# A decoder's mixture-of-depths stage in four sets with side work beside its units, and unread identity products on TensorE

## The reference

```
x = x + L0_attn(ln(x))        # causal self-attention, 16 heads of 16
x = x + L0_xattn(ln(x), ctx)  # cross-attention on 64 context rows
x = x + L0_ffn(ln(x))         # mixture of depths
x = x + L1_attn(ln(x))        # self-attention, RMS-normed q and k
x = x + L1_xattn(ln(x), ctx)  # cross-attention with a mask
x = x + L1_ffn(ln(x))         # 8 experts, top 2
```

```
_, idx = jax.lax.top_k(x @ w_router, 128)
x_sel = take(x, idx);  h = rmsnorm(x_sel, g1)
q, k, v = split(h @ W_qkv.T)              # 16 heads of 16
att = softmax(causal(q k / 4));  x_attn = (att v) @ W_out.T
h2 = rmsnorm(x_sel + x_attn, g2)
x_ff = silu(h2 @ W1.T) * (h2 @ W2.T) @ W3.T     # 682 hidden features
out = x.at[idx].set(x_sel + x_attn + x_ff)
```

## Time and profile before

| | us |
|---|---|
| median of 3 runs | 2638.91 |
| their range | 2628.20 to 2640.23 |
| the profiled execution, its own time | 2641.58 |
| its span in the trace | 2639.9 |
| PE busy | 2316.5 |
| DVE busy | 1453.2 |
| ACT busy | 1130.4 |
| POOL busy | 730.5 |

### The profile page before, as it was taken

How to read it: one execution, slowest core, us unless ns; L and a number is a source line. 1 busy time by engine, 2 the same in 40 slices (tenths; PEclk the granted TensorE clock), 3 DMA queues, 4 the chain that set the end, 5 groups by cost and what they waited for, 6 DMA issues and landing times. The chain is left out here.

```text
span 2639.9 us, 44230 instructions
## 1 busy us (share of the span) xinstructions
PE 2316.5 (88%) x13938; PEld 1441.3 (55%) x13939; DVE 1453.2 (55%) x3873; ACT 1130.4 (43%) x2659; POOL 730.5 (28%) x844
## 2 busy tenths in 40 slices
PE   5999999889984487789999999878898599999998
PEld 2455555445553344423333443345557399999997
DVE  4776766338763324477777767354444834333433
ACT  1665666423331324247777776522232033333332
POOL 3121111144322202232222222053321333333333
PEclk8999999899996799889999999888896799999999
DMA  5233222100002440222222222100007412222221
GB/s 152 86 91 93 74 86 86 35 5 5 5 1 73 52 72 1 48 79 68 68 71 64 66 68 73 37 8 9 6 4 259 145 33 34 36 34 35 35 35 25
DMA packets 134895, 148.76 MB, mean 56 GB/s; under 512 B 25374, under 2 KB 119240, under 8 KB 134600
## 3 DMA queue, kind: packets, MB, share of 16 engines
q1 hardware_dynamic: 119080, 127.23, 16.7%
q0 software_dynamic: 13680, 17.84, 4.2%
q10 hardware_dynamic: 1968, 1.60, 0.5%
HBM read 100.71 MB, written 46.01 MB: 56 GB/s over the span
## 5 line engine op out<-in xcount | busy, mean ns | idle before, releaser
L446 ACT ACTIVATE self_probs<-self_score_ps 128x512 f32<-128x512 f32 (+3 forms) x1024 | 481.1, 516 | 316.1 <-PE self_score_ps L807 163.6
L612 DVE TENSOR_REDUCE self_neg_max<-self_max_ps 128x1 f32<-128x512 f32 x512 | 328.9, 685 | 147.3 <-PE self_max_ps L793 141.9
L793 PE MATMUL self_max_ps<-self_k_stack,self_q_stack 96*128 96x512 bf16 (+3 forms) x1024 | 352.7, 349 | 33.9 <-DVE self_neg_max L609 16.7
L804 PE MATMUL self_score_ps<-self_q_stack,self_k_stack 99*128 99x512 bf16 (+3 forms) x1024 | 343.9, 344 | 1.6 <-ACT self_probs L446 1.6
L2212 ACT ACTIVATE x_stream<-experts_up_ps,experts_bias_now 128x128 f32<-128x128 f32 x568 | 162.0, 368 | 388.0 <-PE experts_up_ps L2433 388.0
L609 DVE CUSTOM_DVE_ANT_0 self_masked<-self_max_ps,self_later 128x128 f32<-128x128 f32 (+3 forms) x512 | 235.2, 488 | 125.6 <-PE self_max_ps L793 114.3
L2433 PEld LDWEIGHTS experts_up_ps<-experts_tileT,x_stream 128*128 128x128 f32 x2272 | 266.9, 193 | 5.0 <-issue 1.5
L2433 PE MATMUL experts_up_ps<-experts_tileT,x_stream 128*128 128x128 f32 x2272 | 267.4, 277 | 1.1 <-DVE x_stream L2349 1.1
L2443 PE MATMUL experts_down_ps<-experts_down,x_stream 128*128 x1136 | 256.8, 380 | 0.0
L818 PE MATMUL self_out_ps<-self_probs,self_values 128*32 128x512 f32 (+3 forms) x2048 | 231.9, 524 | 3.3 <-ACT self_probs L446 1.4
L2443 PEld LDWEIGHTS experts_down_ps<-experts_down,x_stream 128*128 128x128 f32 x1136 | 210.6, 190 | 25.5
(11 more groups left out here) (283 smaller groups left out, 3793.8 us busy)
## 6 DMA issues: line engine op xcount, KB each, us to landing
self_parts_dram<-self_parts SPq DMA_DIRECT2D x64, 384.0 KB, 2.3
self_q_stack<-self_parts_dram SPq DMA_DIRECT2D x384, 64.0 KB, 2.3
self_k_stack<-self_parts_dram SPq DMA_DIRECT2D x360, 64.0 KB, 2.3
experts_up<-moe_up_dram SPq DMA_DIRECT2D x8, 1024.0 KB, 8.2
experts_down<-moe_down_dram SPq DMA_DIRECT2D x8, 1024.0 KB, 10.6
x_stream<-x_dram SPq DMA_DIRECT2D x8, 512.0 KB, 8.3
expert_rows_dram<-experts_down SPq DMA_DIRECT2D x8, 512.0 KB, 6.2
out_dram<-x_stream SPq DMA_DIRECT2D x8, 512.0 KB, 8.2
```

The costliest lines, as they stand in the source:

```text
L446: act.activation(probs[:, i % 8, 0:w], score_ps[:, (16 * n + i) % 3, 0:w], ACT.Exp).then_inc(exp_done, 1)
L612: dve.tensor_reduce(neg_max[:, n % 2, t, h:h + 1], max_ps[:, i % 2, 0:w], AX, ALU.max, negate=True).then_inc(max_read, 1)
L793: last = pe.matmul(max_ps[:, i % 2, 0:w], q_stack[0:ROWS, h, P * t:P * t + P], k_stack[0:ROWS, h, 0:w], start=True, stop=True)
L804: last = pe.matmul(score_ps[:, m % 3, 0:w], k_stack[0:KROWS, head, P * j:P * j + P], q_stack[0:KROWS, head, S - w:S], start=True, stop=not ...
```

## The change

It has three parts.

1. `mixture_of_depths` is written anew. Four sets of two sequences (256 tokens) replace two of four. Sets 0 and 1 are projected at the start (`START`); everything else that is not part of a unit is side work that `beside(i)` assigns to one of 42 steps: X turns rows, Q projects queries and keys of a half (8 heads), V values, O is the output product, T turns the rows for the feed-forward part, H the hidden products, F the third product, B puts back. Every engine runs the same steps. `q_stack` and `k_stack` are double by set, loads are waited for by half (`stacked[s % 2][h]`), the features of a head are permuted on the host (`mod_order`) so that a load takes rows of 4 KB, and a key load takes the same rows 3 or 2 times (`stack_rows`). PSUM has `hidden_ps` of its own; `turned_ps` and `out_ps` have one bank where they had two.
2. Its weights are loaded during cross-attention 0 (SP, at b == 2), and the scaling of the query weights goes there too (POOL, b == 3).
3. `spin` issues products of the identity with itself whose result nobody reads: in the openings of both self-attentions and both cross-attentions, at the end of cross-attention 0, and 24 before the first unit of the rewritten stage.

```diff
+def spin(pe, c, where, count):
+
+    for _ in range(count):
+        pe.matmul(where[:, 0:P], c.ident[:], c.ident[:], start=True, stop=True, skip_group_check=True)
 
...
                     last.then_inc(pv_done, 1)
 
                 start_of_mt = opening.index(("mt", 0))
+                spin(pe, c, out_ps, 20)
                 for use in opening[:start_of_mt]:
+                    if use[0] == "s":
+                        spin(pe, c, out_ps, 4)
                     side_work(*use)
+                spin(pe, c, out_ps, 12)
                 for i in range(16):
                     max_tile(0, i)
+                    spin(pe, c, out_ps, 1)
+                spin(pe, c, out_ps, 3)
                 side_work(*opening[start_of_mt])
                 between = dict(zip((3, 9, 13), opening[start_of_mt + 1:]))
                 for i in range(16):
                     max_tile(1, i)
                     if i in between:
                         side_work(*between[i])
+                    else:
+                        spin(pe, c, out_ps, 1)
                 pe.wait_ge(ones_ready, 2)
                 for n in range(N):
                     b, g = n // NG, n % NG
...
                 for b in range(B):
+                    if routed and b == 2:
+                        for dst, src in router.loads():
+                            sp.dma_start(dst, src).then_inc(depths_loaded, 16)
 
                     wait(sp, v_full, b - 1)
                     sp.dma_start(ctx_one[:, b % 2], ctx_twice[b].rearrange("k p n -> p k n")).then_inc(ctx_loaded[b % 2], 16)
...
@@ -1081,9 +1099,13 @@
                         shift(b + 1, 1)
                     if b + 3 < B:
                         inverse_deviation(b + 3)
+                    if routed and b == 3:
+                        pool.wait_ge(depths_loaded, 16 * len(router.loads()))
+                        pool.tensor_scalar(router.wqkv[:, :, 0:D], router.wqkv[:, :, 0:D], HD ** -0.5, None, ALU.mult).then_inc(depths_scaled, 1)
                 if routed:
                     add_normed(B - 2)
                     add_normed(B - 1)
+                    pool.wait_ge(depths_scaled, 1)
 
             @block.scalar
...
                 WORK = {"xt": turn, "k": keys, "q": queries, "v": value_rows, "ot": turn_out, "ob": turn_back, "e": output,
                         "sr": spread_scores, "bk": turn_pick, "ch": gather, "S": scores, "M": maxima, "PV": with_values}
 
+                idle = {("xt", 0, 0): (out_ps[:, 0], 20), ("M", 0, 0): (out_ps[:, 0], 4), ("M", 0, 2): (out_ps[:, 0], 4)}
+                if routed:
+                    idle.update({("sr", B - 2, 0): (max_ps[:, 0], 8), ("bk", B - 2, 0): (max_ps[:, 0], 8), ("sr", B - 1, 0): (max_ps[:, 0], 16),
+                                 ("bk", B - 1, 0): (max_ps[:, 0], 16)})
                 for step in steps:
+                    if step in idle:
+                        spin(pe, c, *idle[step])
                     m = place.get(step, 0)
                     if m >= 2:
                         pe.wait_ge(*bank_read(*uses[m - 2]))
...
+        START = [("X", 0), ("Q", 0, 0), ("Q", 0, 1), ("V", 0), ("X", 1), ("Q", 1, 0), ("Q", 1, 1), ("V", 1)]
+
+        def beside(i):
+
+            work = []
+            for s in range(2, SB):
+                work += {SETU * (s - 2) + 1: [("X", s)], SETU * (s - 2) + 2: [("Q", s, 0)], SETU * (s - 2) + 3: [("Q", s, 1)],
+                         SETU * (s - 2) + 4: [("V", s)]}.get(i, [])
+            for q in range(B):
+                j = q // BS
+                ff_at = SETU * j + (15, 16)[q % BS]
+                work += {NG * q + 7: [("O", q)], ff_at: [("F", q)], ff_at + 1: [("B", q)]}.get(i, [])
+            for j in range(SB):
+                work += {SETU * j + 13: [("T", j)], SETU * j + 14: [("H", j)]}.get(i, [])
+            return work
+
+        STEPS = SETU * (SB - 1) + 18
+        assert all(not beside(i) for i in (STEPS, STEPS + 1, STEPS + 2, STEPS + 3))
...
+        def stack_rows(s, h, which):
+            stk, item = ((q_stack, 2 * h), (k_stack, 2 * h + 1))[which]
+            for r, count in ((0, 3), (3, 2), (5, 1)):
+                dst = stk[HD * r:HD * (r + count), s % 2, 8 * h:8 * h + 8, :].rearrange("r h t -> r (h t)")
+                if which == 0:
+                    yield dst, scratch[s % 2, item, 0:count].rearrange("c (d h) t -> (c d) (h t)", h=8)
+                else:
+                    yield dst, scratch[s % 2, item, 3 - count].rearrange("(d h) t -> d (h t)", h=8).unsqueeze(0).to_broadcast([count, HD, 8 * T])
 
         with nc.Block() as block:
             @block.sync
             def _(sp):
-                sp.dma_start(wqkv[:], w_qkv.rearrange("(k p) n -> p k n", p=P)).then_inc(loaded, 16)
-                for i, gain in enumerate((gain1, gain2)):
-                    sp.dma_start(gains[:, i], gain).then_inc(loaded, 16)
-                sp.dma_start(wo[:], w_o.rearrange("g p n -> p g n")).then_inc(rest_loaded, 16)
-                sp.dma_start(w1[:], w_1.rearrange("(k p) n -> p k n", p=P)).then_inc(rest_loaded, 16)
-                sp.dma_start(w2[:], w_2.rearrange("(k p) n -> p k n", p=P)).then_inc(rest_loaded, 16)
-                for f in range(FT):
-                    sp.dma_start(w3[0:rows_of(f), f], w_3[P * f:P * f + rows_of(f)]).then_inc(rest_loaded, 16)
                 for s in range(SB):
-                    for i in range(4):
-
-                        sp.wait_ge(part2_cut, 4 * s + i + 1)
-                        wait(sp, stacked, 384 * s)
-                        sp.dma_start(scratch[i], parts[:, i]).then_inc(parts_stored, 16)
-
-                    wait(sp, score_full, UNITS * s)
-                    sp.wait_ge(parts_stored, 64 * s + 64)
-                    for half in range(2):
-                        for stk, item, which in ((q_stack, 2 * half, Q_PART), (k_stack, 2 * half + 1, K_PART)):
-                            for r, part in enumerate(which):
-                                sp.dma_start(stk[HD * r:HD * r + HD, 8 * half:8 * half + 8, :],
-                                             scratch[item, :, part, :].rearrange("(h d) t -> d h t", d=HD)).then_inc(stacked, 16)
+                    for h in range(2):
+                        sp.wait_ge(part2_cut, 2 * s + h + 1)
+
+                        wait(sp, stacked[s % 2][h], 96 * (s // 2))
+                        for item in (2 * h, 2 * h + 1):
+                            sp.dma_start(scratch[s % 2, item].rearrange("c p t -> p c t"), parts[:, item]).then_inc(parts_stored[h], 16)
+                        sp.wait_ge(parts_stored[h], 32 * s + 32)
+
+                        wait(sp, score_full, SETU * (s - 1))
+                        for which in range(1 if s == 0 else 2):
+                            for dst, src in stack_rows(s, h, which):
+                                sp.dma_start(dst, src).then_inc(stacked[s % 2][h], 16)
...
+                def hidden(j):
+                    pe.wait_ge(b_copied, 2 * j + 2)
                     for f in range(FT):
-                        n, r = FT * s + f, rows_of(f)
-                        if f < 2:
-                            pe.wait_ge(exp_done, GH * UNITS * (s + 1))
-                            pe.wait_ge(turned_copied, UNITS * (s + 1))
-                        else:
-                            pe.wait_ge(gated_done, n - 1)
-                        for dst, w in ((score_ps, w1), (turned_ps, w2)):
+                        n, r = FT * j + f, rows_of(f)
+                        wait(pe, gated_done, n - 1)
+                        for i, w in enumerate((w1, w2)):
                             for k in range(KD):
-                                last = pe.matmul(dst[0:r, f % 2], w[:, k, P * f:P * f + r], xT[:, k], start=(k == 0), stop=(k == KD - 1))
+                                last = pe.matmul(hidden_ps[0:r, n % 2, T * i:T * i + T], w[:, k, P * f:P * f + r], xT_b[:, k],
+                                                 start=(k == 0), stop=(k == KD - 1))
                         last.then_inc(hidden_full, 1)
-                    pe.wait_ge(gated_done, FT * s + FT)
-                    for i in range(BS + 1):
...
+                WORK = {"X": turn_rows, "Q": project, "V": value_rows, "O": output, "T": turn_rows2, "H": hidden, "F": output2, "B": put_back}
+
+                for what, *of in START:
+                    WORK[what](*of)
                 pe.wait_ge(constants, 1 + GH)
-                pe.wait_ge(scaled, 1)
-                project(0)
-                pe.wait_ge(rest_loaded, 16 * (3 + FT))
-                attend(0)
-                project(1)
-                feed_forward(0)
-                attend(1)
-                feed_forward(1)
+                spin(pe, c, out_ps, 24)
+                for i in range(STEPS):
+                    if i < UNITS:
+                        scores(i)
+                    if 0 <= i - 2 < UNITS:
+                        turn_probs(i - 2)
+                    if 0 <= i - 3 < UNITS:
+                        with_values(i - 3)
```

(11 more changed lines are left out.)

559 lines of the change are left out of this document (285 added, 274 removed).

## The result

The changed kernel takes 2598.05 us in the median of four runs (2591.28 to 2605.26), the kernel before 2637.62; the ratio is 0.9857, 95% interval 0.9818 to 0.9896. That is 1.4% faster, 15 us above the forecast of 2583 and inside its range. A later measurement of the same two kernels gave 0.9855 (0.9832 to 0.9879).

A forecast was written before the change was run, and what follows sets the result against it. TensorE's idle and half-clock time bounds the rewritten stage: 30 opening + 146 work + 34.6 stalls = 210.6 us, 45.7 less; unread products elsewhere save 11. From 2641.6 that gives 2585, as a median 2583, range 2563 to 2612.

The forecast's parts named there:

- The new opening: Start of rewritten stage: weights already loaded, first score at about 30 us (27 to 35), where it was 53.7.
- Later sets have 8 steps as cover: Stack loads of later sets: 8 steps, some 40 us, cover even slow key loads.
- Rival 3: Key loads copying a block run on few DMA engines, 15 us a half; 26 us lost, 2609; chance 0.13.
- They lie beside the second half's load: The 24 unread products before the first score, 5 to 10 us, are covered; at most some 5 us if not.
- The loop: Rewritten stage behind its opening: 146 us of TensorE work at full clock in 42 steps, plus 34.6 us of stalls.
- 256 columns cost 0.43 us; the output product, 4 of 256, agrees: Price of a TensorE product at full clock; 256 such products in the rewritten stage make 110 us.
- What moved into cross 0 costs nothing: Twelve DMA issues on SP and one POOL scaling moved into cross 0: no cost, 1.5 us without slack.
- Unread products outside, 11 us (5 lost to 17 won): Outside the rewritten stage they keep TensorE's clock up: two thirds of a 16.5 us gain taken, 11 us.
- Rival 2: Unread products change nothing outside the new stage, the clock having fallen again before it is needed: 2594; chance 0.15.
- Rival 5: Each of 48 side pieces waits for ACT or DVE: gain gone at 1.2 us a piece, 2655 at 1.5; chance 0.03.
- The signs to look for: Profile: first score at 30 us, stage 205 to 217, T waits 2 to 4 us, key loads under 8, clock above 0.85.

The follow-up runs named there:

- sp_keys: Changed kernel with SP, not ACT, issuing set 0's key loads too, behind the query loads; ratio to the kernel before 0.9830.
- no_spins: Changed kernel without any unread products (empty `spin`), those ahead of the first unit included; ratio to the kernel before 0.9889.
- spins_only: Kernel before plus the unread products outside the rewritten stage, old mixture of depths kept; ratio to the kernel before 0.9938, 16.4 us.
- early_and_late: Changed kernel with SP issuing all key loads, none copying, and T, H, F and B one step later; ratio to the kernel before 0.9786.
- sp_split: Changed kernel with SP issuing all key loads, each 16 rows made once, none copying; 2580.1 us, ratio to the kernel before 0.9796.
- split_keys: Changed kernel with the copying key loads split into 3 and 2 loads of 16 rows, ACT still issuing set 0's; ratio to the kernel before 0.9831.

## Why the prediction came out as it did

The time was in the range and on the right side, by two errors that partly cancel, which is luck: the rewritten stage gave 19 us less than forecast, and the unread products elsewhere about 5 to 10 more. By the profiles that leaves 9 of the 15 us. The other 6 lie between an execution and the median: I took off 2.7 us for it, and the changed kernel's profiled execution was itself 3.8 us under its median. Of the 19 us, 8.7 are the opening, 8.7 the loop, and 1.6 a slip of the sum: the 256.3 us of before run on to the start of the next stage, and my 210.6 end at the last product (1085.56 in the kernel before, where the next stage starts at 1087.2).

- **The new opening: the step that failed.** "The first score starts at about 30 us (27 to 35)". It started at 38.7. My sum had each engine's durations right (the first half's part 2 was ready at 12.8 us, forecast 12; the first loads left at 15.6), but let TensorE project set 1 in the meantime and left out that ACT's issues wait in its list. Every cut of set 1 hangs behind them. `sp_keys` shows 26.0 without that.
- **"Later sets have 8 steps as cover"**: right, no unit of sets 1 to 3 waited for a stack. But I priced a slow load only by when its own data is late. Rival 3 named the mechanism, and the runs agree with it: 26 us was its price, and it cost 10 together with ACT's place, for the most part by the stores behind such loads.
- **"They lie beside the second half's load"**: wrong for the 24 unread products; they stood behind ACT's wait and cost 1.6 us net (`no_spins`).
- **The loop.** Stalls 34.6, measured 25 behind the first score; T's waits 10.8, as forecast. The work was sized at 146 us and took 164. The granted clock was 0.95 over 189 us, that is half clock for some 18 us, which costs up to 9 us of work (an estimate); I had put no half clock into the loop but for the tail. Stalls and half clock together are then some 34 us, as many as I had forecast of stalls alone. The other 9 us are the price of a product. "256 columns cost 0.43 us; the output product, 4 of 256, agrees": it did not, 1.84 / 4 is 0.46, and the rows below give 0.50 for the third product (6 products in 3.02 us) and 0.46 for the hidden ones (16 in 7.30). With some 230 such products behind the first score, 0.04 us each is 9 us. A long row of 512 columns at 0.43 per 256 leaves out what each short group costs at its end (inside a group the records start 0.216 us apart, which is 0.43 a product). This term was mis-sized, and a row in front of me said so.

```profile
914.47 7.30 PE L1963 MATMUL depths_hidden_ps<-depths_xT_b,depths_w 128*128 128x256 f32 x32 [0.52 <-DVE depths_gated L1830]
...
1046.50 1.99 PE L1982 MATMUL depths_general<-depths_delta,depths_back 128*128 128x256 f32 x8 [0.52 <-DVE depths_delta L1834]
...
1048.50 3.02 PE L1972 MATMUL depths_general<-depths_w,depths_gated 128*128 128x256 f32 x12
```

- **What moved into cross 0 costs nothing**: no cost shows, but the 1.5 us that I named as its bound could not be seen in a scatter of 8. That it brings the stage nothing much either (3 us) I had not weighed; the forecast tied it to the early start.
- **Unread products outside, 11 us (5 lost to 17 won)**: measured 16.4 (11 to 21). Self 0, cross 0 and self 1 gave 1.6, 2.0 and 3.2 in `spins_only`, 6.8 together, where two thirds of 4, 5.5 and 4 are 9; cross 1 gave 10 to 13 in the profiles where two thirds of 3 stood. So the sum came out by a gain that no term of mine held. I had read only the rows that the products precede, and the gain lies in the 250 us behind. Rival 2 is refuted.
- **Rival 5**: no step of the loop had more than 3.2 us of wait; refuted.
- **The signs to look for**: T's waits came as named; the clock at the edges passed 0.85 in two of the three stretches above, the cross end had 0.76; "no DMA wait of more than 5 us" held for TensorE's own waits and hid the 13 us that ACT had. Key loads "that land in under 8 us": the changed kernel's trace shows no landing for them; in `sp_keys`, with the same loads, those of set 0's second half took 9.1.

## What to carry to other kernels

An engine that issues a DMA behind a semaphore wait holds all of its later work: give such issues to a queue that does nothing else, and when that moves the wait, look for what holds the new place before calling it off; here two edits gave 10.0 us together, and -1.2 and 2.6 apart. Count for a DMA not only when its data is needed but what is queued behind it. And where TensorE loses its clock over and over, compare whole stages, not the rows beside the edit, and more than one execution: with a few microseconds of work at the stage's start the 250 us behind it took 11 us less, and a like stage with nothing edited moved by up to 8 between executions.

## What was not expected of the hardware

- Two kernels with the same cross 1 stage had the same stage time to 0.1 us (295.7 and 295.7), and those with unread products ahead came in two groups, 282.3 to 282.7 and 285.1 to 286.0. The code of cross 1 does not tell the groups apart: the changed kernel (282.5) and `early_and_late` (285.5) are equal there. In cross 0 equal code and equal openings were followed by 278.2, 281.5 and 286.2 us, at a granted clock of 0.97, 0.96 and 0.93. Such stages take one of a few times, and which one is not set by the kernel alone.
- Stores of 2 x 192 KB took 2.8 us to land ahead of all loads, 7 to 9.5 right behind loads that copy a block, and 2.8 to 3.7 behind single-copy loads of the same rows in `sp_split`; one in `split_keys` took 5.1.
- Eight unread products (3.62 us at half clock) ahead of the pick and the gather at 798.40 left both at half clock; sixteen (5.25 us, half clock for the first part) ahead of those at 821.93 had them at full clock.
